# Row maxima in one transfer and head loads in five: three attention layers of a nine-stage kernel

## The reference

```
decay:   scores = (q k^T / sqrt(256)) * exp(-0.01 |i - j|);  softmax;  attn v;  W_o
rope:    q, k rotated by rotary tables; scores = q k^T / 4;  softmax;  attn v;  W_o
latent:  q = x; k, v through a 128-wide bottleneck; rotary;  softmax;  attn v;  w_o + b_o
```

## Time and profile before

| | us |
|---|---|
| median of 3 runs | 3668.29 (3661.93 to 3672.26) |
| profiled execution | 3668.39, of it the span 3666.7 |
| PE busy | 2727.7 (74% of the span) |
| DVE busy | 1900.5 (52%) |
| ACT busy | 1488.6 (41%) |
| POOL busy | 972.2 (27%) |
| mean granted TensorE clock | 0.864 of full speed |

### The profile page before, as it was taken

How to read it: one execution, slowest core, us unless ns; L and a number is a source line. 1 busy time by engine, 2 the same in 40 slices (tenths; PEclk the granted TensorE clock), 3 DMA queues, 4 the chain that set the end, 5 groups by cost and what they waited for, 6 DMA issues and landing times. The chain is left out here.

```text
span 3666.7 us, 44234 instructions
## 1 busy us (share of the span) xinstructions
PE 2727.7 (74%) x14004; PEld 1432.3 (39%) x14004; DVE 1900.5 (52%) x4849; ACT 1488.6 (41%) x2903; POOL 972.2 (27%) x997
## 2 busy tenths in 40 slices
PE   4557877777755489999956597699268888885994
PEld 2223433333344133333335365466123333324663
DVE  4535655555454577777743444111567777752112
ACT  1234555554542255666553332111036655561110
POOL 1224444333223133222203310300422233203003
PEclk7678989888978699999987798799679999995997
DMA  5253323333115212222114300332222112202223
GB/s 174 74 192 94 92 77 88 88 96 92 46 64 170 73 57 63 73 62 62 53 39 132 109 1 1 126 113 75 76 76 64 62 57 64 72 19 99 103 103 103
DMA packets 166008, 300.85 MB, mean 82 GB/s; under 512 B 22960, under 2 KB 120689, under 8 KB 161056
## 3 DMA queue, kind: packets, MB, share of 16 engines
q1 hardware_dynamic: 150288, 248.50, 21.7%
q0 software_dynamic: 15504, 49.68, 4.1%
HBM read 203.21 MB, written 104.47 MB: 84 GB/s over the span
## 5 line engine op out<-in xcount | busy, mean ns | idle before, releaser
L1526 DVE CUSTOM_DVE_ANT_0 decay_junk<-decay_scores_q,decay_corr 128x512 bf16<-128x512 f32 x512 | 337.9, 688 | 371.7 <-PE decay_scores_q L1290 370.6
L1451 ACT ACTIVATE decay_probs<-decay_scores_k 128x512 f32<-128x512 f32 x512 | 300.6, 601 | 402.6 <-PE decay_scores_k L1309 355.1
L1529 DVE TENSOR_REDUCE rope_mx<-rope_scores_q 128x1 f32<-128x512 f32 x512 | 326.0, 683 | 153.3 <-PE rope_scores_q L1290 153.3
L1529 DVE TENSOR_REDUCE latent_mx<-latent_scores_q 128x1 f32<-128x512 f32 x512 | 326.2, 683 | 148.1 <-PE latent_scores_q L1290 148.0
L1451 ACT ACTIVATE latent_probs<-latent_scores_k 128x512 f32<-128x512 f32 x512 | 292.1, 599 | 251.2 <-PE latent_scores_k L1303 249.7
L1451 ACT ACTIVATE rope_probs<-rope_scores_k 128x512 f32<-128x512 f32 x512 | 292.9, 599 | 247.5 <-PE rope_scores_k L1303 246.2
L1306 PE MATMUL decay_scores_k<-decay_QS,decay_KS 99*128 99x384 bf16 (+3 forms) x512 | 161.1, 316 | 174.0 <-DMA decay_QS<-decay_mT 151.6
L1290 PE MATMUL decay_scores_q<-decay_KS,decay_QS 96*128 96x512 bf16 x512 | 217.2, 425 | 76.1 <-DVE decay_mx L1526 51.1
L1290 PE MATMUL latent_scores_q<-latent_KS,latent_QS 96*128 96x512 bf16 x512 | 205.2, 403 | 47.3 <-DVE latent_mx L1529 26.7
L1290 PE MATMUL rope_scores_q<-rope_KS,rope_QS 96*128 96x512 bf16 x512 | 206.5, 405 | 32.3 <-DMA rope_QS<-rope_parts_dram 16.2
L1665 POOL TENSOR_SCALAR_AFFINE_SELECT decay_probs<-decay_probs 128x512 f32<-128x512 f32 x128 | 89.1, 696 | 508.7 <-ACT decay_probs L1451 508.7
(11 more groups left out here) (451 smaller groups left out, 5591.9 us busy)
## 6 DMA issues: line engine op xcount, KB each, us to landing
decay_parts_dram<-decay_parts SPq DMA_DIRECT2D x64, 384.0 KB, 2.7
experts3x_w<-in_w_dram SPq DMA_DIRECT2D x16, 1024.0 KB, 7.9
experts4x_w<-in_w_dram SPq DMA_DIRECT2D x16, 1024.0 KB, 7.9
decay_KS<-decay_parts_dram SPq DMA_DIRECT2D x64, 192.0 KB
decay_QS<-decay_parts_dram SPq DMA_DIRECT2D x64, 192.0 KB
rope_parts_dram<-rope_parts SPq DMA_DIRECT2D x32, 384.0 KB, 3.1
latent_parts_dram<-latent_parts SPq DMA_DIRECT2D x32, 384.0 KB, 2.6
decay_KS<-decay_parts_dram SPq DMA_DIRECT2D x64, 128.0 KB
```

The source lines that it names most:

```text
L1451: act.activation(probs[:, (b * 16 + kk) % PSLOTS, h, :], psB[:, s % 2, :], ACT.Exp, scale=scale).then_inc(exp_done, 1)
L1526: dve.tensor_tensor_reduce(junk[:, a % 2, :], psA[:, A_BANK[k], :], corr[:, qt, :], 1.0, -3.0e38, ALU.mult, ALU.max, mx[:, grp % 2, qt, h: ...
L1529: dve.tensor_reduce(mx[:, grp % 2, qt, h:h + 1], psA[:, A_BANK[k], :], AX.X, ALU.max).then_inc(a_done, 1)
```

## The change

There are four parts.

1. `max_rows` moves the twelve partitions of `mT` into three partitions of `QS` in one transfer for each scaling, where there were three of one partition each.
2. `load_group` has five transfers for each scaling instead of six. The parts of `q` are stored in the opposite order (`part`), so that the six products can be laid out in another way: `KS` 0 to 63 is one pair of parts read twice, `QS` 0 to 31 and 32 to 63 are one part each read twice, and the last 32 partitions of both are two parts that are not neighbours.
3. On SP's queue `max_rows` of group 2 stands ahead of load 0, in `decay` with the fifth parts write between. The maxima and their split are two steps sooner (`SPAN`, `SPLIT_BEFORE`), and `Wo0`, `Wo1` go from steps 17 to 19 to steps 31 to 35.
4. `Vraw` and `lay_values` are gone: ACT writes the values straight into one of two `Vaug` buffers.

```diff
-    SPAN, SPLIT_BEFORE = (-26, -11), -10
+    SPAN, SPLIT_BEFORE = (-28, -13), -12
-                (14, "aT1"), (17, "Wo0"), (18, "Wo1"), (22, "OT0"), (24, "mT2"), (26, "v0"), (28, "v1"), (38, "OT1"),
+                (14, "aT1"), (22, "OT0"), (24, "mT2"), (26, "v0"), (28, "v1"), (32, "Wo0"), (35, "Wo1"), (38, "OT1"),
...
-    ROW_DMAS = 3 * NV
+    ROW_DMAS = NV
...
-        Vraw, Vaug = sb("Vraw", [P, 4, D], F32), sb("Vaug", [P, 4, H, 32], F32)
+        Vaug = sb("Vaug", [P, 2, 4, H, 32], F32)
...
+        def part(nb, j, i):
+
+            return parts[:, (nb * NCH + j) % RING, i if CHAINS[j][0] == "k" else 2 - i, :]
...
+                def heads_of(first, step, n):
+
+                    src = scr[first:first + step * (n - 1) + 1:step].rearrange("s (d h) t -> s d h t", d=16)
+                    return src[:, :, h0:h0 + 4, :].rearrange("s d h t -> s d (h t)")
+
                 for v in range(NV):
-                    for at, n in ((0, 3), (48, 2), (80, 1)):
-                        dst = KS[at:at + 16 * n, v, c, h0:h0 + 4, :].rearrange("p h t -> p (h t)")
-                        src = scr[bass.ds(part_of(nb, "k", c, v), n)].rearrange("s (d h) t -> s d h t", d=16)
-                        src = src[:, :, h0:h0 + 4, :].rearrange("s d h t -> (s d) (h t)")
-                        sp.dma_start(dst, src).then_inc(grp_loaded[grp], 16)
-                for v in range(NV):
-                    for part, (at, n) in enumerate(((0, 3), (48, 2), (80, 1))):
-                        dst = QS[at:at + 16 * n, v, c, h0:h0 + 4, :].rearrange("p h t -> p (h t)")
-                        one = scr[bass.ds(part_of(nb, "q", c, v) + part, 1)].rearrange("s (d h) t -> (s d) h t", d=16)
-                        one = one[:, h0:h0 + 4, :].rearrange("d h t -> d (h t)")
-                        src = one.unsqueeze(0).to_broadcast([n, 16, 4 * S]) if n > 1 else one
-                        sp.dma_start(dst, src).then_inc(grp_loaded[grp], 16)
+                    ks = KS[0:96, v, c, h0:h0 + 4, :].rearrange("p h t -> p (h t)")
+                    qs = QS[0:96, v, c, h0:h0 + 4, :].rearrange("p h t -> p (h t)")
+                    k, q = part_of(nb, "k", c, v), part_of(nb, "q", c, v)
+                    sp.dma_start(ks[0:64], heads_of(k, 1, 2).unsqueeze(0).to_broadcast([2, 2, 16, 4 * S])).then_inc(
+                        grp_loaded[grp], 16)
+                    for at, one in ((0, q + 1), (32, q + 2)):
+                        sp.dma_start(qs[at:at + 32], heads_of(one, 1, 1).to_broadcast([2, 16, 4 * S])).then_inc(
+                            grp_loaded[grp], 16)
+                    sp.dma_start(ks[64:96], heads_of(k, 2, 2)).then_inc(grp_loaded[grp], 16)
+                    sp.dma_start(qs[64:96], heads_of(q, 2, 2)).then_inc(grp_loaded[grp], 16)
...
                 for v in range(NV):
-                    for s in range(3):
-                        sp.dma_start(QS[96 + s:97 + s, v, c, h0:h0 + 4, :], mT[4 * s:4 * s + 4, :]).then_inc(
-                            rows_loaded, 16)
+                    sp.dma_start(QS[96:99, v, c, h0:h0 + 4, :], mT[:, :]).then_inc(
+                        rows_loaded, 16)
...
                 for j in range(HALF_CHAINS):
                     write_parts(b + 1, j)
+                max_rows(tag, b, b, 2)
+                if decay:
+                    write_parts(b + 1, HALF_CHAINS)
                 load_group(b + 1, 0)
-                max_rows(tag, b, b, 2)
-                for j in range(HALF_CHAINS, NCH):
+                for j in range(HALF_CHAINS + (1 if decay else 0), NCH):
                     write_parts(b + 1, j)
                 load_group(b + 1, 1)
...
-                    if not (isinstance(nb, int) and nb == 0):
-                        act.wait_ge(vaug_done, nb)
-                    ins_ = act.copy(Vraw[:, 2 * n:2 * n + 2, :].rearrange("p t d -> p (t d)"), psM[:, m, :])
+                    if nb > 1:
+                        act.wait_ge(pv_done, (nb - 1) * 16)
+                    ins_ = act.copy(Vaug[:, nb % 2, 2 * n:2 * n + 2, :, 0:16],
+                                    psM[:, m, :].rearrange("p (t h d) -> p t h d", t=2, d=16))
...
-                    if s == 2:
-                        lay_values(tag, b)
```

More of the change, by code:

```diff
@@ L981, in mha_layer @@
         USES = [(0, "xT0"), (1, "xT1"), (3, "k0"), (5, "q0"), (6, "OT3"), (8, "mT1"), (10, "aT0"), (11, "k1"), (13, "q1"),
-                (14, "aT1"), (17, "Wo0"), (19, "Wo1"), (21, "OT0"), (24, "mT2"), (26, "v0"), (28, "v1"), (37, "OT1"),
+                (14, "aT1"), (21, "OT0"), (24, "mT2"), (26, "v0"), (28, "v1"), (31, "Wo0"), (34, "Wo1"), (37, "OT1"),
                 (40, "mT3"), (53, "OT2"), (56, "mT0")]
@@ L987, in mha_layer @@
         USES = [(0, "xT0"), (1, "xT1"), (3, "k0"), (6, "OT3"), (8, "mT1"), (10, "aT0"), (11, "k1"), (14, "aT1"),
-                (17, "Wo0"), (19, "Wo1"), (21, "OT0"), (24, "mT2"), (26, "v0"), (28, "v1"), (37, "OT1"), (40, "mT3"),
+                (21, "OT0"), (24, "mT2"), (26, "v0"), (28, "v1"), (31, "Wo0"), (34, "Wo1"), (37, "OT1"), (40, "mT3"),
                 (53, "OT2"), (56, "mT0")]
@@ L1104, in mha_layer @@
         e_ready, e_exp, sel_done = sem("e_ready"), sem("e_exp"), sem("sel_done")
-        vaug_done, pv_done, o_taken = sem("vaug_done"), sem("pv_done"), sem("o_taken")
+        pv_done, o_taken = sem("pv_done"), sem("o_taken")
         rec_done = sem("rec_done")
@@ L1137, in first_part @@
             wait_parts(eng, nb, j)
-            eng.tensor_copy(parts[:, (nb * NCH + j) % RING, 0, :], fc[:, j % 2, :]).then_inc(p0_done, 1)
+            eng.tensor_copy(part(nb, j, 0), fc[:, j % 2, :]).then_inc(p0_done, 1)
             eng.wait_ge(p0_done, nb * NCH + (j + 1))
-            eng.tensor_tensor(rr[:, (nb * NCH + j) % RING, :], fc[:, j % 2, :], parts[:, (nb * NCH + j) % RING, 0, :], ALU.subtract).then_inc(r1_done, 1)
+            eng.tensor_tensor(rr[:, (nb * NCH + j) % RING, :], fc[:, j % 2, :], part(nb, j, 0), ALU.subtract).then_inc(r1_done, 1)
         def last_part(eng, nb, j):
             eng.wait_ge(p1_done, nb * NCH + (j + 1))
-            eng.tensor_tensor(parts[:, (nb * NCH + j) % RING, 2, :], rr[:, (nb * NCH + j) % RING, :], parts[:, (nb * NCH + j) % RING, 1, :],
+            eng.tensor_tensor(part(nb, j, 2), rr[:, (nb * NCH + j) % RING, :], part(nb, j, 1),
                               ALU.subtract).then_inc(p2_done, 1)
@@ L1284, in max_scores @@
                 if a == 0:
-                    pe.wait_ge(grp_loaded[grp], (nb + 1) * (16 * 6 * NV))
+                    pe.wait_ge(grp_loaded[grp], (nb + 1) * (16 * 5 * NV))
                 if not (isinstance(nb, int) and nb * 64 + A_LAST[k] < 0):
@@ L1326, in value_sums @@
                 if kk == 0:
-                    pe.wait_ge(vaug_done, b + 1)
+                    for of in ("v0", "v1"):
+                        at = ("pre", 0, of) if b == 0 else ("first" if b == 1 else "mid", b - 1, of)
+                        pe.wait_ge(m_taken[bank(*at)], emptied(*at))
                 if kt == 0 and not (isinstance(b, int) and b * 4 + grp < 1):
@@ L1332, in value_sums @@
                     for h in range(4):
-                        pe.matmul(psO[32 * h:32 * h + 32, kt * P:(kt + 1) * P], Vaug[:, kt, 4 * grp + h, :],
+                        pe.matmul(psO[32 * h:32 * h + 32, kt * P:(kt + 1) * P], Vaug[:, b % 2, kt, 4 * grp + h, :],
                                   low[:, kk % 2, h, :], start=False, stop=False)
                 for h in range(4):
-                    last = pe.matmul(psO[32 * h:32 * h + 32, :], Vaug[:, kt, 4 * grp + h, :],
+                    last = pe.matmul(psO[32 * h:32 * h + 32, :], Vaug[:, b % 2, kt, 4 * grp + h, :],
                                      probs[:, (b * 16 + kk) % PSLOTS, h, :], start=(kt == 0), stop=(kt == 3))
@@ L1339, in value_sums @@
                     for h in range(4):
-                        last = pe.matmul(psO[32 * h:32 * h + 32, 0:P], Vaug[:, kt, 4 * grp + h, :],
+                        last = pe.matmul(psO[32 * h:32 * h + 32, 0:P], Vaug[:, b % 2, kt, 4 * grp + h, :],
                                          low[:, kk % 2, h, :], start=False, stop=False)
@@ L1424, in middle_part @@
                 wait_parts(act, nb, j)
-                act.copy(parts[:, (nb * NCH + j) % RING, 1, :], rr[:, (nb * NCH + j) % RING, :]).then_inc(p1_done, 1)
+                act.copy(part(nb, j, 1), rr[:, (nb * NCH + j) % RING, :]).then_inc(p1_done, 1)
             for name in ORDER["pre"][:2]:
@@ L1545, in split_maxima @@
                 dve.tensor_tensor(mp[:, :, 2, :], mr[:, :, :], mp[:, :, 1, :], ALU.subtract).then_inc(ms_done, 1)
[L1547 to L1558, removed]
             def normalise_heads(tag, b, nb, name):
@@ L1648, in _ @@
                 pool.wait_ge(ones_set, v + 1)
-            nc.gpsimd.memset(Vaug[:, :, :, 16:32], 1.0).then_inc(ones_set, 1)
+            nc.gpsimd.memset(Vaug[:, :, :, :, 16:32], 1.0).then_inc(ones_set, 1)
             pool.wait_ge(ones_set, NV + 1)
```

## The result

The changed kernel takes 4241.13 us (median, 4233.68 to 4250.13), the kernel before 3667.47: the ratio is 1.157 (95% interval 1.154 to 1.160). The span of its profiled execution is 4232.0 us instead of 3666.7. The forecast was 4160.

What follows compares the result with a forecast made beforehand. PE waiting in `decay` for rows of maxima, stuck behind head loads partly confined to two DMA engines, was the bound; `decay` +335, `rope` +75, `latent` +69 on 3668.39 gave 4147, stated as 4160 us, range 4010 to 4310.

Steps and rivals of the forecast that it cites:

- the rule of the Trainium skill: DMA engines used: the largest number up to 16 dividing the slowest dimension larger than 1 of both access patterns.
- the old broadcasts: Kernel before, transfers into `QS` with source outer extents of 3 or 2: claimed to run on 3 and 2 engines.
- Rival A: Head loads: only broadcasts are confined, stepped sources might spread; 21 us a `decay` load, 3746 us in all; chance 0.06.
- rival B: Head loads spread over 16 engines, 6.6 us a `decay` load, waits for rows mostly go; 3495 us; chance 0.05.
- both waits: Each `decay` batch before: PE waits for rows of maxima, 7.38 us ahead of step 32 and 10.75 ahead of 48.
- The sum: Forecast's added terms: `decay` +335, `rope` +75, `latent` +69, total +479 on 3668.39, giving 4147 us.
- The bare gap between step 16 and the issue of load 0: Middle `decay` batch: 19.5 us plus 1.4 until parts are made, less projections of 3.59 + 1.89, leaves 15.4.
- the hand-overs: `decay` gap: 2 us for half clock after a long wait, 2.7 for landing, semaphore and first packet.
- the same bookkeeping: Sum of a `decay` batch's waits, made for the kernel before: some 6 us less waiting than the rows show.
- The first tile: Start of `decay`: all four loads in line from 70.66, first tile at 200 instead of 141.70, +58 us.
- the term that was mis-sized: `rope` and `latent`, step 48 waits for load 1 and group 3's rows: +7 us a batch in `rope`, 6 in `latent`.
- The sign named for this layer: Profile after, stated for `rope`: one wait of about 6 us at step 48 and a batch near 82.
- a gap and a wait: `decay`: load 3 to load 0 gap, less the moved projections; maxima need load 0 at step 36, about 1.5 us a batch.

Runs made afterwards that it cites:

- the first experiment: Changed kernel with the sixteen dimensions as outer extent of every head-load source, six transfers per scaling, same bytes: 3462.13 us, ratio 0.925 to the kernel before.

## Why the prediction was right, and where it was short

**The cause.** That "each of the five new loads would run on 2" engines held. It rested on a share of 0.13 in the kernel before; the share of 0.13 in the changed kernel and the run with the loads turned round (0.72 in the window of a load, ratio 0.925) show it. This is the rule of the Trainium skill ("DMA: Bandwidth & Descriptors", section "Why a DMA increments its semaphore by 16 and not by 1") at work, and the stepped transfers, on which the trace of before was silent, obey it too. For the old broadcasts the rows of the prediction show two engines only, not the 3 that it also reads from the trace; the same trace has them at 574 to 576 us, with a share of 0.19 (3/16) and 72 GB/s. Rival A (3746) and rival B (3495) fell with that. B is what the change would have been with the other layout. Its mechanism was right, since with the loads spread both waits vanished, but 3495 was too careful by 110 us (0.923 x 3667 = 3385): it had nothing for the new steps, which are worth 1.4%, some 50 us, and a `decay` batch became 22 us shorter where the two waits were 18.

**Decay.** The sum gave a load of 29.7 us and a middle batch of 147; measured are 30.5 and 143 to 146. The difference is in the packets: 192 of them on each engine in 30.5 us are 0.159 us for one, where the sum had 0.155. The bare gap between step 16 and the issue of load 0 was put at 15.4 us and is 15.0 (695.89 to 710.93). With the hand-overs it was put at 20 and then raised to 25, because the same bookkeeping fell 6 us short on the kernel before. That raise was wrong here: from step 16 to step 36 are 48.9 us, and less a load of 30.5 that leaves 18.4. The first tile was to come at 200 and came here:

```profile
207.35 0.27 PE L1314 MATMUL decay_scores_k<-decay_QS,decay_KS 99*128 99x128 bf16 x1 [45.85 <-DMA decay_QS<-decay_mT]
```

Batch 0 took 167 instead of 159, and the last one 79, 9 more than before. Together `decay` cost 338 us more; the sum said 335. So close a sum is in part luck: the sum had the start and batch 0 together 15 us too short, and the six middle batches 12 us too long (882, where they took 870).

**Rope and latent, the term that was mis-sized.** The sum gave 82.5 us a batch for `rope` and one less for `latent`, and they take 87 to 90 in `rope` and 85 to 88 in `latent`. The step that failed is that load 1 "is issued at 48.5 in the batch", and that it lands, with the rows of group 3 behind it, at 66. It took the two engines to be free by then. SP's and PE's rows of `latent`, a batch that begins at 3444.26, show otherwise:

```profile
3478.99 0.56 SPq L1189 DMA_DIRECT2D latent_KS<-latent_parts_dram  x1
...
3488.40 3.53 SPq L1189 DMA_DIRECT2D latent_KS<-latent_parts_dram  x1
```

```profile
3497.77 0.61 PE L1298 MATMUL latent_scores_q<-latent_KS,latent_QS 96*128 96x512 bf16 x1 [6.01 <-DMA latent_QS<-latent_parts_dram]
...
3514.98 0.61 PE L1311 MATMUL latent_scores_k<-latent_QS,latent_KS 99*128 99x512 bf16 x1 [5.33 <-DMA latent_QS<-latent_mT]
```

Load 0 is issued 34.7 us into the batch and lands at 53.5, a wait of 6.0 at step 36 that the sum hadn't. The sign named for this layer was one wait, at step 48, and there are two. Load 1 was issued earlier than I said, at 44.1, but the engines were only free for it when load 0 had landed, and it landed 17.2 us after that, at 70.7 instead of 66. That is some 4 us a batch. Over the seven batches that follow one another `rope` takes 82.5 us more than before and `latent` 74.0, where the sum had 48 and 42, so 67 are missing. The starts of the two layers (from the first head load to the first tile) came to 32.1 and 30.8 more instead of 27 each, another 9, and their last batches, which the sum left out, are 7 longer. With the 3 of `decay` that is 86, all but one of what the profiled execution has over 4147. The forecast of 4160 had allowed 13 of it, and the median is 7 above the profiled execution; so it was short by 81. Had I followed load 0 through the batch as I did in `decay`, 4 us a batch more would have brought the forecast near 4217, by an estimate from this one batch.

**The rest.** The moved rows, the values and the transfers of rows were taken at 0 under the loads, which can't be checked in the changed kernel; without the slow loads they are worth 0.4%, nothing and 0.25%. The moved projections and the earlier maxima were only credited to a gap and a wait, and with fast loads the two together are worth more than any of these, 1.4%.

## What to carry to other kernels

Before a transfer is reshaped, look at the outermost extent of its source, and not only at how many bytes or transfers there are: the kernel with five transfers of an outer extent of 2 took 1.25 times as long as the one with six of 16. (The runs varied the source's extent; what the destination's does they don't show.) A DMA share that stays flat at a few sixteenths while something waits, here 0.13 or 2/16, is the sign. Here it was cured by turning two dimensions round, which is possible where the order on the partitions is free, as it is along a contraction. And when a queue's time per item grows, follow every item through one period in each stage, also in those where the mean load is still below the bound.

## What the runs showed of the hardware

- Two engines moved 52 to 53 GB/s, some 26 each, for 20 us at a time; that figure carried over from the kernel before to the changed one within 3% (30.5 us a load against 29.7). It didn't matter whether the source repeats a part or steps over one.
- SP's issues take longer while much of what it issued before hasn't landed: of the changed kernel's first loads one pair of issues took 8.53 us where the pair before took 1.30 (start, us, queue, line, transfer, count). In the first experiment each of the twelve issues of load 0 takes 0.6 us.

```profile
72.20 1.30 SPq L1192 DMA_DIRECT2D decay_QS<-decay_parts_dram  x2
...
75.84 8.53 SPq L1192 DMA_DIRECT2D decay_QS<-decay_parts_dram  x2
```

- Chips differ in some stages only. The changed kernel's profiled execution had a span of 4232.0 us on one and 4318.3 on another, while `decay`, the first of the three stages, ended within 5 us of the same time (1334.3 and 1338.7). Most of the rest is in the two small routed layers: writing their results takes 75 and 77 us on the one chip (first to last issue) and 100 us each on the other.
